# Lowering the planned durations of eight VectorE steps in a kernel whose instruction order is made by a list scheduler

## What is computed

```python
def _ssd_scan(q, k, v, a, eps):
    def step(carry, inp):
        S, z = carry
        qt, kt, vt, at = inp
        S = at[..., None, None] * S + kt[..., :, None] * vt[..., None, :]
        z = at[..., None] * z + kt
        num = jnp.einsum('bhk,bhkv->bhv', qt, S)
        den = jnp.einsum('bhk,bhk->bh', qt, z) + eps
        return ((S, z), num / den[..., None])
# q = elu(x @ Wq) + 1, k = elu(x @ Wk) + 1, v = x @ Wv,
# a = sigmoid(x @ Wa + ba + 2); attention = scan(q, k, v, a) @ Wo
# ffn: rows of lhs and columns of rhs scaled by their absmax / 127, rounded,
#      multiplied as integers, scaled back
x = x + _layernorm(attention(_layernorm(x)))
x = x + _layernorm(ffn(_layernorm(x), rhs))
```

## Time and profile before

| | us |
|---|---|
| runs timed | 1210.03 and 1141.07 |
| their median | 1175.55 |
| profiled execution | 1140.54 |
| its span, slowest core (core 1) | 1139.0 |
| spans of the 8 cores | 1124.3 to 1139.0 |
| mean granted TensorE clock of the cores | 0.893 to 0.910 |

### The profile page before, as it was taken

One profiled execution on the slowest core, in us unless ns is written; L12 is line 12 of the kernel. 1 busy time (PEld: TensorE's weight loads), 2 busy tenths in 40 slices (PEclk: granted clock), 3 DMA queues, 4 the chain that ended last, 5 costly groups with the idle time before them and its releaser, 6 DMA issues.

```text
span 1139.0 us, 18886 instructions; the slowest of 8 cores (1124.3 to 1139.0 us)
## 1 busy us (share of the span) xinstructions
PE 819.3 (72%) x5532; PEld 417.8 (37%) x5532; DVE 775.9 (68%) x1820; ACT 705.4 (62%) x1417; POOL 61.3 (5%) x94
## 2 busy tenths in 40 slices
PE   0026876969788797879787878788797978797412
PEld 0012433434344444444443434344444434444200
DVE  3448988577776858585858586677758685858350
ACT  0036447686859585868585686858485858675332
POOL 1200000000000000101010000000010101000000
PEclk9999897999989897989898999989888989898766
DMA  9995214444426362624344534444262535342312
GB/s 200 206 157 104 62 20 102 68 109 75 103 56 131 50 136 39 140 46 85 93 86 96 80 93 74 104 73 114 52 134 39 107 80 92 85 76 75 56 54 38
DMA packets 159723, 102.16 MB, mean 90 GB/s; under 512 B 138883, under 2 KB 139142, under 8 KB 159622
## 3 DMA queue, kind: packets, MB, share of 16 engines
q1 hardware_dynamic: 146038, 63.17, 26.2%
q0 software_dynamic: 13584, 37.79, 18.8%
HBM read 42.24 MB, written 33.55 MB: 67 GB/s over the span
## 4 chain that ended last, share of the span: by engine, by line
PE 41%; DMA 16%; ACT 15%; issue 14%; DVE 12%; POOL 1%; DVEq 0%; ACTq 0%; POOLq 0%; SPq 0%
PE pbs L597 13%; PE pbs L1079 12%; PE pbs L893 7%; DMA s_xs<-x 5%; DMA s_xnf<-s_xn 3%; DMA s_qlf<-s_ql 3%; PE pbs L773 2%; ACT s_x2d L949 2%; ACT s_ffn_f L1094 2%; DVE s_ql L1064 2%; DMA s_Wq<-wq 2%; DMA s_Wv<-wv 2%; DVE s_scm L780 1%; PE pb L679 1%; PE pb L682 1%
## 5 line engine op out<-in xcount | busy, mean ns | idle before, releaser
L597 PE MATMUL pbs<-s_Wq,s_xnf 128*128 128x512 bf16 x512 | 126.0, 402 | 55.4 <-DMA s_xnf<-s_xn 33.6
L1079 PE MATMUL pbs<-s_QR,s_qlf 128*128 128x512 bf16 x512 | 144.3, 432 | 27.8 <-DMA s_qlf<-s_ql 25.4
L893 PE MATMUL pbs<-s_Wo,s_ofm 128*128 128x512 bf16 x512 | 121.2, 385 | 27.1 <-DMA s_ofm<-s_otok 13.8
L597 PE MATMUL pbs<-s_Wv,s_xnf 128*128 128x512 bf16 x512 | 120.2, 384 | 7.4 <-ACT s_e_sb L633 7.3
L597 PE MATMUL pbs<-s_Wk,s_xnf 128*128 128x512 bf16 x512 | 117.3, 379 | 6.2 <-ACT s_ffn_f L911 5.9
L780 DVE TENSOR_TENSOR s_scm<-pbs,s_mask 128x512 bf16<-128x512 f32 x128 | 82.1, 681 | 31.7 <-PE pbs L773 31.2
L597 PEld LDWEIGHTS pbs<-s_Wq,s_xnf 128*128 128x128 bf16 x512 | 50.3, 102 | 123.5 <-issue 74.4
L1079 PEld LDWEIGHTS pbs<-s_QR,s_qlf 128*128 128x128 bf16 x512 | 52.2, 107 | 94.0 <-issue 58.2
L893 PEld LDWEIGHTS pbs<-s_Wo,s_ofm 128*128 128x128 bf16 x512 | 47.2, 98 | 87.1 <-issue 38.1
L1094 ACT ACTIVATE s_ffn_f<-pbs 128x1024 f32<-128x1024 f32 x32 | 32.8, 1024 | 67.6 <-PE pbs L1079 67.6
L597 PEld LDWEIGHTS pbs<-s_Wk,s_xnf 128*128 128x128 bf16 x512 | 49.1, 98 | 63.6 <-issue 7.4
(11 more groups left out here) (172 smaller groups left out, 1926.2 us busy)
## 6 DMA issues: line engine op xcount, KB each, us to landing
y<-s_x2d SPq DMA_DIRECT2D x32, 512.0 KB, 6.3
s_xs<-x SPq DMA_DIRECT2D x32, 256.0 KB, 6.9
s_xs<-x POOLq DMA_DIRECT2D x32, 256.0 KB, 5.6
y<-s_fn POOLq DMA_DIRECT2D x16, 512.0 KB, 5.8
y<-s_o_n POOLq DMA_DIRECT2D x16, 512.0 KB, 6.0
s_o_n<-rhs SPq DMA_DIRECT2D x8, 512.0 KB, 6.8
s_fn<-rhs POOLq DMA_DIRECT2D x4, 512.0 KB, 9.2
s_Wq<-wq POOLq DMA_DIRECT2D x2, 1024.0 KB, 16.9
```

The lines of the kernel that those rows point to most:

```text
L597: last = e.matmul(pb[bank_i][:, :], sb["xnf" + s][:, kc * 128:(kc + 1) * 128], sb[W][:, kc * 1024 + gidx * 512:kc * 1024 + (gidx + 1) * 51 ...
L893: last = e.matmul(pb[bank_i][:, 0:c1 - c0], sb["ofm"][:, kc * 128:(kc + 1) * 128], sb["Wo"][:, kc * 1025 + c0:kc * 1025 + c1], start=(kc = ...
L1079: last = e.matmul(pb[bank_i][:, 0:c1 - c0], sb[qfn][:, kc * 128:(kc + 1) * 128], sb["QR"][:, kc * 1025 + c0:kc * 1025 + c1], start=(kc == ...
```

## The change

The planned duration `est` of eight kinds of VectorE step becomes 5 ns less: 345 becomes 340 and 650 becomes 645. Nothing else differs. Steps by the line at which the profile shows them: L619 and L639 (min of elu), L813, L867 (345 to 340), L788, L874, L878 and L1049 (650 to 645).

```diff
@@ elu_evac_k, L619 and the same in elu_evac, L639
                 sb[dst][:, :], sb["e_sb"][:, :], 1.0),
-                reads=["e_sb", "e_h0"], writes=[dst], est=345)
+                reads=["e_sb", "e_h0"], writes=[dst], est=340)
@@ scan_chunk, L788
-            reads=[St, "rep" + s], writes=["Szb"], est=650)
+            reads=[St, "rep" + s], writes=["Szb"], est=645)
@@ L813
-                reads=["pb%d" % bank, "rep" + s], writes=["Pg_%d" % bank], est=345)
+                reads=["pb%d" % bank, "rep" + s], writes=["Pg_%d" % bank], est=340)
@@ L867
-                    writes=["ot_b%d_%d" % (bank, side)], est=345)
+                    writes=["ot_b%d_%d" % (bank, side)], est=340)
@@ L874
-            reads=[St, "rep" + s, "Szb"], writes=[St], est=650)
+            reads=[St, "rep" + s, "Szb"], writes=[St], est=645)
@@ L878
-             reads=[St, "Pg_2", "Pg_3"], writes=[St], est=650)
+             reads=[St, "Pg_2", "Pg_3"], writes=[St], est=645)
@@ tail_pair, L1049
                 writes=["qtb", "wrep", "wrep_h0"],
-                est=650)
+                est=645)
```

## The result

The changed kernel takes 1149.91 us (median of 18 runs), the kernel before 1141.47 (median of 17 on the same chip). The ratio is 1.0069, with a 95% interval of 1.0049 to 1.0088; a few disturbed runs of both kernels (such as 1213.78 and 1220.59 us) are left out of the ratio. So the change costs about 0.7%, 8 us. The forecast was 1140 and "no change": the time lies inside its range and within 2%, but it did move, and to the slower side.

The account below looks back on a forecast made before the run. The prediction took a relay between engines, TensorE nearest the limit, to bound the kernel. It summed 1140.5 us (span 1139.0 and 1.5 around it) + 0 + 0 = 1140.5, rounded 1140, range 1118 to 1170.

Parts of the forecast that it names:

- Durations and work: All engines: only planned numbers change, no instruction, tile, wait rule or DMA, so every duration stays; 0 us.
- The swap of L743, the tie and the price 0: VectorE: chains of L867 and L743 tie at 680, so L743 goes first in every pair, idle time covering it; 0 us.
- bounds of 9 and 10 us: Limits for L743's swap over 15 pairs: 10.4 us lost without its cover, at best 9.2 us won.
- The large bounded places: TensorE's waits at L799 for L707 (44.9 us) and at L825 for Szb (16.6 us), bounding what reordering is worth.
- The two rivals built on these: Quantising step ahead of value chain: 1158 or 1176 us, chance 0.22; value chain ahead: 1122 or 1106 us, chance 0.15.
- the second comparison: VectorE, scan L568 against Szb of L788: L568's lead grows from 0.5 to 15.5 ns, no swap; at most 16.6 us.
- Readiness, taken as 0: Whether a step is ready when its engine is free: could not be followed, bounded by 18 us either way, priced 0.
- The argument for 0: Two alternating orders of pairs have nearly the same TensorE idle time, 10.95 and 10.23 us, so reordering was priced 0.
- the alternation changes into one repeated order: Rival: one kind of pair remains, 30 us either way; counted half to the slower (0.22), half to the faster rival (0.15).
- the signs that the forecast is right: Equal counts and mean durations, L743 ahead of four L867, VectorE idle before L780, steady two-pair period, L799's wait near 45 us.
- The two-pair period: Time of two successive tail pairs in the repeated part, forecast to stay at 120 to 122 us.
- the signs that it is wrong: A 1.2 us step newly before L707, L799 or L825 waits growing or vanishing, TensorE groups reordered, one kind of pair.

Follow-up runs that it names:

- sum_later: Changed kernel with ScalarE's pass L519 moved behind the elu's last relu (L636) in ten pairs; ratio 0.9965 to the kernel before.
- sum_sooner: Kernel before with ScalarE's pass L519 moved ahead of the elu in five pairs, 25 ScalarE places; ratio 1.0115 to the kernel before.
- late15: Kernel before with the new planned durations only in tail pair 15 and fronts of chunks 30 and 31; 1136.05 us against 1142.71, ratio 0.9939.
- both_later: late15 with ScalarE's passes L519 and L522 moved behind the elu in seven odd pairs; ratio 1.0050 to the kernel before.
- wo_later: Changed kernel with the second half of Wv (L597) ahead of the odd chunk's Wo groups (L893), pairs 1 to 14; ratio 1.0152 to the kernel before.
- wo_first: Changed kernel with the even chunk's first Wo group (L893) ahead of the odd chunk's L799, pairs 1 to 14; ratio 1.0216 to the kernel before.

## Why the prediction was wrong

**Durations and work: right.** Counts are equal, and VectorE's and ScalarE's busy time moved by 1.4 and 4.0 us. (One figure beside it is off: 5 ns is 1.4% of a step of 345, not under 1%.)

**The swap of L743, the tie and the price 0: right.** The swap is in the trace where it was put, VectorE's idle time before L780 (2.10 us) covers it, and alone it measures 1.0002, within bounds of 9 and 10 us.

**The large bounded places: right at L799, not at Szb.** L799's wait stayed at 45.1 us, and no quantising step passed the value chain. The two rivals built on these did not happen. At the second comparison the forecast was "no swap", from the length of the chains. But in every second pair of the kernel before, L788 already stood behind the scan L568 of the other chunk, and after it stands ahead of it in all pairs but two: TensorE's wait for Szb, 16.6 us in 7 places, is 5.0 us in 2 and gone from the repeated pairs. This too came by readiness and not by the chains. Most of it came back as L825's wait for L813, which grew from 12.0 to 20.7 us.

**Readiness, taken as 0: the step that failed.** The forecast said that this could not be followed and bounded it by 18 us, then took 0. In its place stood: several hundred places moved, L519 ahead of the elu in every pair instead of in every second (about +12 us by sum_later, +13 for five harsher places by sum_sooner), and another last pair (-7 us by late15, 0.61% of 1142.71). +12 and -7 leave 5 of the measured 8 us; the rest is not attributed, and the intervals of these ratios are 2 to 4 us to each side. The size was inside the bounds, the sign was not to be had from them.

**The argument for 0: misread.** It said that two quite different orders alternate and hardly differ in idle time (10.95 against 10.23 us). That cut lies where one kind has 366 matmuls and the other 326, and idle time of one kind is counted in the other's stretch. At a cut with equal work the same trace has 11.38 against 9.53 us in the mean over pairs and cores, 61.07 against 59.60 us. A pair of one kind is 1.5 us longer. Had that been read, the rival "the alternation changes into one repeated order" would have had the price 12 pairs / 2 x 1.5 = 9 us slower if the worse kind remained. That is of the size of the 15 us that the repeated pairs lost; the forecast had put half of this rival to each side, so that it cancelled. The reading could not have told which kind remains.

**The end: not looked at.** 52.0 us lie behind the last cut with TensorE busy for 9.58 of them, and TensorE's wait of 12.98 us for one transfer stands just ahead of it. No step of the prediction put a price on it, and the gain of 6.7 us came from pair 14 on.

**The signs named.** Of the signs that the forecast is right, the counts, L743 ahead of the four L867 with VectorE idle behind them, and L799's 45 us all held. The two-pair period did not stay at 120 to 122 us, it is 2 x 61.58 = 123.2. That sign was a weak one, since in the kernel before two of seven such periods on core 1 take 124.1 and 123.1 us. Of the signs that it is wrong, three came: one kind of pair instead of two, waits of L825 that vanish (Szb) and grow (L813), and TensorE groups in another order.

## What to carry to other kernels

In a kernel whose order a planner writes, a duration changed by 5 ns is a new order, and it has to be read as one: compare, engine by engine, what now stands ahead of what, and look first for a step that waits for a transfer and has work for another engine behind it. The total of such a wait did not tell here (ScalarE waited 37.6 us for x before and 36.2 after); what stands behind it, and whether that was ready, decides. Moving a step is no safe repair: both_later, wo_later and wo_first each removed a wait and lost time. Cut a periodic trace where each stretch holds the same work, and read the end apart from the repeated part: here +15 and -7 us made +8, and the best kernel took only the second (0.9939).

## What the runs showed of the hardware

**The price of a wait of TensorE does not end with the wait.** Busy time in stretches with the granted clock (the figure after POOL), for the two groups of Wv matmuls of sum_sooner, behind 4.05 us of waiting:

```profile
423.92:427.03 3.11, 3.11 (x9) 1.02 (x9) 2.67 (x7) 3.02 (x9) 0.00 (x0) 0.57 0.39 158
427.35:429.09 1.74, 1.74 (x10) 0.79 (x10) 1.28 (x7) 0.71 (x3) 0.00 (x0) 1.00 0.00 0
```

for the last group of late15, behind 7.82 us:

```profile
1057.74:1063.88 6.14, 6.14 (x16) 2.07 (x16) 0.00 (x0) 0.00 (x0) 0.00 (x0) 0.58 0.31 59
```

for the same group of before, behind 12.98 us:

```profile
1077.40:1082.78 5.38, 5.38 (x16) 1.85 (x16) 0.00 (x0) 0.00 (x0) 0.00 (x0) 0.67 0.00 0
```

and for sixteen matmuls of after, behind 1.18 us:

```profile
532.05:535.67 3.62, 3.62 (x17) 1.65 (x18) 1.41 (x6) 1.48 (x3) 0.85 (x1) 1.00 0.70 91
```

The clock is at the 2.4 GHz level all through behind 1.18 us, and for most of the group at the 1.2 GHz level behind 4.05 and 7.82 us (0.57 and 0.58). Eight matmuls cost 3.18 us there where the next eight cost 1.90, so 1.3 us are paid behind the wait of 4.05. The loss isn't in proportion to the wait. Behind 12.98 us on this core the figure is 0.67. Over the cores with whole records it is 0.55 to 0.67 behind 13 to 15 us in before, and over all cores 0.58 to 0.73 behind 8 us in late15, so one group on one core ranks nothing. The Trainium skill, TensorE: Matmul & The Clock Gate, Part 1, has half the clock as the state without activity, which activity ends; the rows agree, with 0.57 and then 1.00. This fits sum_sooner's loss of 13 us, of which the idle time is only a part: on cores 4 to 7 twelve pairs have 7.0 us more of it (12 x 0.58) and 6.0 us more busy time (50.17 against 49.67 us a pair). The shorter waits of after raise the busy time by 1.9 us only in the whole span (815.1 to 817.0, mean of the cores). What part of the 6.0 us is the clock was not separated.

**Half of the chip at a third level.** In the profiled execution of sum_sooner cores 0 to 3 were granted 0.8125 of the clock for 118 to 214 us in all, cores 4 to 7 never. TensorE was busy 838.6 us on the former and 819.8 on the latter in the mean, with the same order; in before it was 815.3 and 815.0. On core 1 this lay behind 951 us, so the rows of this core shown above are not of it. A stretch of it (PE's clock is the 0.81):

```profile
1000.00:1050.00 50.00, 47.44 (x260) 22.51 (x261) 29.70 (x78) 33.06 (x66) 1.74 (x2) 0.81 0.38 69
```

What set the level was not looked into.

**How finely the order matters.** The thirteen kernels timed against the kernel before run the same instructions in other orders, and lie between 0.994 and 1.022 of it.
